# A two-layer decoder on one core: the feed forward begun in the tail of cross attention, with three smaller reorderings

## What is computed

```
x = x + gated_delta_net(layernorm(x))                # layer 0: recurrent attention, 8 heads
x = x + cross_attention0(layernorm(x), ctx, mask)    # 16 heads of 16
x = x + mixture_of_experts(layernorm(x))             # top 2 of 8 experts
x = x + self_attention(layernorm(x))                 # layer 1: causal, one head of 256
x = x + cross_attention1(layernorm(x), ctx, mask)    # 16 heads of 16, with biases
h = silu(xn @ w1 * s1) * (xn @ w2 * s2)              # xn = layernorm(x); ternary weights, 1024 hidden
h = gelu(h @ h1 * t1)                                # h1, h2: 1024 x 1024
h = gelu(h @ h2 * t2)
out = x + h @ w3 * s3
```

## Time and profile before

| what | value |
|---|---|
| executions (3) | 2084.59, 2084.89, 2089.97 us |
| profiled execution, its own time | 2085.05 us |
| its span in the trace | 2083.7 us |
| PE busy | 1951.1 us (94%) |
| DVE / ACT / POOL busy | 1124.0 / 689.5 / 624.0 us |
| mean granted TensorE clock | 0.981 of full |
| chain of waits, by engine | PE 78%, DVE 13%, issue 4%, ACT 2%, POOL 1%, DMA 1% |

### The profile page before, as it was taken

How to read it: one execution, slowest core, us unless ns; L and a number is a source line. 1 busy time by engine, 2 the same in 40 slices (tenths; PEclk the granted TensorE clock), 3 DMA queues, 4 the chain that set the end, 5 groups by cost and what they waited for, 6 DMA issues and landing times.

```text
span 2083.7 us, 38336 instructions
## 1 busy us (share of the span) xinstructions
PE 1951.1 (94%) x14432; PEld 1233.8 (59%) x14432; DVE 1124.0 (54%) x3161; ACT 689.5 (33%) x1720; POOL 624.0 (30%) x647
## 2 busy tenths in 40 slices
PE   6699999999888999998999899999889999999998
PEld 3467777777665666665445566666545545545545
DVE  6988888887655677676665566666520010100100
ACT  3134443443334555552001356555510110111100
POOL 3323333233104666663000266666500000000000
PEclk9899999999999999999999999999989999999999
DMA  5121211112103101010000000000030000000000
GB/s 171 26 26 23 33 21 27 29 20 28 15 11 114 34 24 34 23 32 10 0 0 1 9 27 19 26 19 27 2 162 0 9 0 0 9 0 0 9 0 9
DMA packets 126007, 53.73 MB, mean 26 GB/s; under 512 B 108680, under 2 KB 117760, under 8 KB 125056
## 3 DMA queue, kind: packets, MB, share of 16 engines
q1 hardware_dynamic: 125824, 51.27, 10.0%
HBM read 45.38 MB, written 5.85 MB: 25 GB/s over the span
## 4 chain that ended last, share of the span: by engine, by line
PE 78%; DVE 13%; issue 4%; ACT 2%; POOL 1%; DMA 1%; SPq 0%; DVEq 0%; ACTq 0%; POOLq 0%
PE ps L2103 19%; PE ps L515 6%; PE ps L1281 5%; PE ps L2090 5%; PE ps L1788 4%; PE ps L1303 4%; PE ps L1337 4%; PE ps L1358 3%; PE ps L1319 3%; PE ps L578 3%; PE ps L2111 3%; PE ps L639 2%; DVE big_b L783 2%; PE ps L1414 2%; PE ps L1290 1%
## 5 line engine op out<-in xcount | busy, mean ns | idle before, releaser
L1703 POOL TENSOR_TENSOR h_w<-h_w 125x336 int32<-125x336 int32 x384 | 337.5, 908 | 232.7 <-ACT h_w L1498 232.6
L1597 DVE CUSTOM_DVE_ANT_0 h_w<-ps,h_w 112x375 f32<-112x375 f32 x512 | 263.3, 543 | 3.1 <-PE ps L1281 3.0
L783 DVE SCALAR_TENSOR_TENSOR big_b<-ps,taps,big_b 128x444 f32<-128x444 f32 (+2 forms) x288 | 194.0, 674 | 26.8 <-ACT big_b L707 10.8
L1498 ACT ACTIVATE h_w<-ps 125x336 f32<-125x336 f32 x512 | 197.6, 468 | 22.2 <-PE ps L1303 22.2
L2103 PE MATMUL ps<-big_a,h_w 128*128 128x448 f32 x512 | 193.5, 540 | 3.7 <-DVE big_a L2150 3.7
L2103 PE MATMUL ps<-big_b,h_w 128*128 128x448 f32 x512 | 193.5, 540 | 0.7 <-ACT big_b L2129 0.7
L2158 DVE TENSOR_TENSOR xn<-ps,w_s 112x512 f32<-112x512 f32 x8 | 5.2, 686 | 299.4 <-PE ps L2111 299.4
L249 POOL TENSOR_TENSOR rstd<-var_eps,minus_half 112x4 f32<-112x4 f32 x12 | 12.1, 1011 | 488.4 <-DVE var_eps L236 488.4
L2103 PEld LDWEIGHTS ps<-big_a,h_w 128*128 128x128 f32 x512 | 97.0, 190 | 100.3 <-issue 93.7
L2103 PEld LDWEIGHTS ps<-big_b,h_w 128*128 128x128 f32 x512 | 96.9, 190 | 95.6 <-issue 93.7
L1303 PEld LDWEIGHTS ps<-h_w 32*125 32x125 f32 x3072 | 97.3, 185 | 61.9 <-issue 61.0
(11 more groups left out here) (230 smaller groups left out, 3385.5 us busy)
## 6 DMA issues: line engine op xcount, KB each, us to landing
h_w<-in_h SPq DMA_DIRECT2D x2, 4096.0 KB, 16.9
kq_w<-in_ctxT SPq DMA_DIRECT2D x16, 375.0 KB, 3.1
h_w<-in_ctxT SPq DMA_DIRECT2D x16, 375.0 KB, 3.3
h_w<-in_mask SPq DMA_DIRECT2D x16, 164.1 KB, 3.4
kq_w<-in_kq_w SPq DMA_DIRECT2D x8, 256.0 KB, 3.1
w<-in_vz_w SPq DMA_DIRECT2D x8, 256.0 KB, 3.4
blocks<-h_w SPq DMA_DIRECT2D x128, 12.2 KB
expert_w<-in_expert_w SPq DMA_DIRECT2D x1, 2048.0 KB
```

What stands on the lines that cost most here:

```text
L783: dve.scalar_tensor_tensor(p3(dst)[:, :, i:], p3(ps[:, bank, 0:GT])[:, :, 0:T - i], k.taps[:, h, n, TAPS - 1 - i:TAPS - i], p3(dst)[:, :, ...
L1498: act.activation(k.PTx[(4 * Q + r) % RING], ps[0:CK, turned_bank(Q, r), 0:NC * T], ACT.Exp).then_inc(s["exp"], 1)
L1597: dve.tensor_tensor_reduce(k.masked[r % 2], ps[0:T, score_bank(Q, r), 0:S2], k.mask_add[n % 2], -1.0, 3.0e38, ALU.add, ALU.min, k.neg_max[ ...
L1703: pool.tensor_tensor(P.bitcast(I32), P.bitcast(I32), k.mask_I[n % 2], ALU.mult).then_inc(s["weights"], 1)
```

## The change

Four edits.

1. **Feed forward begun in the tail.** In layer 1's cross attention the norm of feed forward's group 0 is done in the last sequence, in the places where layer 0 has the experts' norm (both of its copies on DVE). The first `BEGUN_FFN = 3` gate tiles are put at the ends of steps (B, 1), (B, 2) and (B, 3) on PE, two silus behind the copy of `oa` in (B, 2) on ACT, two products in (B, 2) and (B, 3) on DVE. In step (B, 1) `add_output(B - 2)` moves behind DVE's `weights`. PE's waits for `c_x` at the stage's start are gone; one stands now ahead of the next group's transposes. SP no longer waits for `c_x` ahead of h1 and h2, which have a semaphore each; `k.inv` gets memory of its own. `output_turn` and `output_back` of sequence B-2 wait for the norm's copies.
2. **Self-attention's norm on other banks.** Queries go to banks 4 and 5 and keys to 2 and 3 (`QK_BANKS`; before, queries had 2 and 3), and the next group's transposes go to banks 2 and 3, behind the waits for the copied queries and keys and no longer behind the copied values; that wait moves to `project_v`. PE's wait for `moe_x` moves from the stage's start to behind the first two projections, which use banks 4 and 5.
3. **First mask first.** `mask_rows(0)` stands ahead of the loop, so ahead of the first maxima, in both layers.
4. **Output by pairs.** `y_ps`, `y` and `ffn_x` count pairs of sequences: DVE scales and adds a pair when its products are done, SP sends eight transfers of two sequences where there were four of four.

```diff
@@ memory @@
+    k.inv = sb("inv", [T, XH])[:, :]
-    k.inv = room(XH, 1, parts=T)
@@ cross_pe: output_turn, output_back, early, loop @@
             pe.wait_ge(s["V"], 2 * n + 4)
             if l == 0:
                 pe.wait_ge(s["lnT_act"], LN_MOE + 1)
+            else:
+                pe.wait_ge(s["lnT_dve"], LN_FFN + 1)
...
-        if l == 0 and seq == B - 2:
-            pe.wait_ge(s["lnT_dve"], LN_MOE + 1)
+        if seq == B - 2:
+            pe.wait_ge(s["lnT_dve"], (LN_MOE + 1, LN_FFN + KD)[l])
...
-        elif l == 0 and (seq, q) == (B - 1, 2):
+        elif (seq, q) == (B - 1, 2):
             pe.wait_ge(s["V"], 2 * (n + 1))
-            ln_pe_half(pe, k, s, LN_MOE, 0, 7)
+            ln_pe_half(pe, k, s, LN_NEXT[l], 0, 7)
-        elif l == 0 and (seq, q) == (B - 1, 3):
+        elif (seq, q) == (B - 1, 3):
             pe.wait_ge(s["on"], n)
-            ln_pe_half(pe, k, s, LN_MOE, 1, 7)
+            ln_pe_half(pe, k, s, LN_NEXT[l], 1, 7)
...
+        elif l and (seq, q) == (B, 1):
+            pe.wait_ge(s["w_ffn"], 64)
+            pe.wait_ge(s["lnT_dve"], LN_FFN + KD)
+        if l and step in range(B * QUADS + 1, B * QUADS + 1 + BEGUN_FFN):
+            ffn_pe_gate(pe, k, s, 0, step - B * QUADS - 1)
@@ cross_act @@
+            elif l and seq == B:
+                act.wait_ge(s["w_ffn"], 64)
+                ffn_act_gate(act, k, s, 0, 0)
+                ffn_act_gate(act, k, s, 0, 1)
@@ cross_dve @@
+    mask_rows(0)
...
-        if q == 1 and is_sequence(seq - 2) and not (l == 0 and seq == B):
+        if q == 1 and is_sequence(seq - 2) and seq < B:
             add_output(seq - 2)
...
+        if l and (seq, q) in ((B - 1, 2), (B - 1, 3)):
+            ln_copy(dve, k, s, LN_FFN, q - 2, 7, k.xT[:, q - 2, :], "lnT_dve")
...
-        if q == 0 and seq == 0:
-            mask_rows(0)
...
+        elif (seq, q) == (B - 1, 0):
+            ln_dve_stats(dve, k, s, LN_FFN, 0)
+        elif (seq, q) == (B - 1, 1):
+            dve.wait_ge(s["xnT"], 2 * B)
+            ln_dve_scale(dve, k, s, LN_FFN, 0)
+        elif (seq, q) == (B, 1):
+            add_output(seq - 2)
+        elif (seq, q) == (B, 2):
+            dve.wait_ge(s["w_ffn"], 64)
+            ffn_dve_gate(dve, k, s, 0, 0)
+        elif (seq, q) == (B, 3):
+            ffn_dve_gate(dve, k, s, 0, 1)
@@ cross_pool @@
-        elif l == 0 and (seq, q) == (B - 1, 1):
-            ln_pool(pool, k, s, LN_MOE)
+        elif (seq, q) == (B - 1, 1):
+            ln_pool(pool, k, s, LN_NEXT[l])
@@ attention_pe @@
+QK_BANKS = (4, 5, 2, 3)
...
         for n in range(2 * KD):
+            if g == 0 and n == KD:
+                pe.wait_ge(s["moe_x"], 32 * NG)
             for c in range(KD):
-                ins = pe.matmul(ps[:, 2 + n, 0:GT], k.attn_w[:, c, n * 128:(n + 1) * 128], k.xT[:, c, :],
+                ins = pe.matmul(ps[:, QK_BANKS[n], 0:GT], k.attn_w[:, c, n * 128:(n + 1) * 128], k.xT[:, c, :],
...
-    pe.wait_ge(s["moe_x"], 32 * NG)
...
-        if more:
-            pe.wait_ge(s["v_sb"], g + 1)
-            ln_pe(pe, k, s, LN_ATTN + g + 1, 6)
         pe.wait_ge(s["q_sb"], 2 * (g + 1))
         pe.wait_ge(s["kk_sb"], 2 * (g + 1))
+        if more:
+            ln_pe(pe, k, s, LN_ATTN + g + 1, 2)
...
         if more:
+            pe.wait_ge(s["v_sb"], g + 1)
             project_v(g + 1)
@@ ffn_sp @@
-    sp.wait_ge(s["c_x"], 2 * B)
     sp.wait_ge(s["PV"], 2 * B * QUADS)
     for n in range(2):
-        sp.dma_start(k.hw[n][:, :, :], a[f"h{n + 1}"]).then_inc(s["hidden_w"], 16)
+        sp.dma_start(k.hw[n][:, :, :], a[f"h{n + 1}"]).then_inc(s[f"hidden_w{n}"], 16)
     for g in range(NG):
-        sp.wait_ge(s["ffn_x"], g + 1)
-        sp.dma_start(out[g].rearrange("b t d -> t b d"), k.x[:, g * G:g * G + G, :]).then_inc(s["out_done"], 16)
+        for n in range(2):
+            sp.wait_ge(s["ffn_x"], 2 * g + n + 1)
+            sp.dma_start(out[g, 2 * n:2 * n + 2].rearrange("b t d -> t b d"),
+                         k.x[:, g * G + 2 * n:g * G + 2 * n + 2, :]).then_inc(s["out_done"], 16)
@@ ffn_pe @@
+def ffn_pe_gate(pe, k, s, g, m):
+    if m >= 2:
+        pe.wait_ge(s["h0"], nth(g, HT, m - 2))
+    elif g:
+        pe.wait_ge(s["y"], 2 * g)
+    for n in range(2):
+        for c in range(KD):
+            ins = pe.matmul(k.ps[:, 2 + 2 * n + m % 2, 0:GT], ...)
+        ins.then_inc(s["w12"], 1)
...
-    pe.wait_ge(s["w_ffn"], 64)
-    pe.wait_ge(s["c_x"], 2 * B)
-    ln_pe(pe, k, s, LN_FFN, 6)
     for g in range(NG):
-        pe.wait_ge(s["lnT_dve"], LN_FFN + KD * g + KD)
+        if g:
+            pe.wait_ge(s["lnT_dve"], LN_FFN + KD * g + KD)
+        for m in range(0 if g else BEGUN_FFN, HT):
+            ffn_pe_gate(pe, k, s, g, m)
...
-                    pe.wait_ge(s["hidden_w"], 32)
+                if m == 0:
+                    pe.wait_ge(s[f"hidden_w{n}"], 16)
...
+                if g == 0:
+                    pe.wait_ge(s["c_x"], 2 * B)
                 ln_pe(pe, k, s, LN_FFN + g + 1, 6)
...
-        ins.then_inc(s["y_ps"], 1)
+            if j % 2:
+                ins.then_inc(s["y_ps"], 1)
@@ ffn_dve @@
-        dve.wait_ge(s["y_ps"], g + 1)
-        for n in range(G // 2):
...
+        for n in range(2):
+            dve.wait_ge(s["y_ps"], 2 * g + n + 1)
+            dve.tensor_tensor(y[:, 2 * n:2 * n + 2, :], two(ps[0:T, 4 + n, :]),
+                              k.w3_s[:, :].unsqueeze(1).to_broadcast([T, 2, D]), ALU.mult).then_inc(s["y"], 1)
+            dve.wait_ge(s["y"], 2 * g + n + 1)
+            xs = k.x[:, g * G + 2 * n:g * G + 2 * n + 2, :]
+            dve.tensor_tensor(xs, xs, y[:, 2 * n:2 * n + 2, :], ALU.add).then_inc(s["ffn_x"], 1)
```

More of the change, by code:

```diff
@@ L1085 @@
 POOL_BANKS = 6
+LN_NEXT = (LN_MOE, LN_FFN)
 def is_sequence(c):
@@ L1982, in queries @@
             act.wait_ge(s["qk"], nth(g, 4, n))
-            act.activation(qk[:, n, :], ps[:, 2 + n, 0:GT], ACT.Copy, scale=1.0 / 16).then_inc(s["q_sb"], 1)
+            act.activation(qk[:, n, :], ps[:, QK_BANKS[n], 0:GT], ACT.Copy, scale=1.0 / 16).then_inc(s["q_sb"], 1)
     def values(g):
@@ L2023, in attention_dve @@
         if g < NG - 1:
-            ln_copy(dve, k, s, LN_ATTN + g + 1, 1, 7, k.xT[:, 1, :], "lnT_dve")
+            ln_copy(dve, k, s, LN_ATTN + g + 1, 1, 3, k.xT[:, 1, :], "lnT_dve")
         dve.wait_ge(s["A_S"], g + 1)
@@ L2059, in attention_pool, with ffn_act_gate, ffn_dve_gate @@
     cross_norm_pool(pool, k, s, 1, 0)
+BEGUN_FFN = 3
 def ffn_sp(sp, k, s, a, out):
-    sp.wait_ge(s["c_x"], 2 * B)
     sp.wait_ge(s["PV"], 2 * B * QUADS)
     for n in range(2):
-        sp.dma_start(k.hw[n][:, :, :], a[f"h{n + 1}"]).then_inc(s["hidden_w"], 16)
+        sp.dma_start(k.hw[n][:, :, :], a[f"h{n + 1}"]).then_inc(s[f"hidden_w{n}"], 16)
     for g in range(NG):
-        sp.wait_ge(s["ffn_x"], g + 1)
-        sp.dma_start(out[g].rearrange("b t d -> t b d"), k.x[:, g * G:g * G + G, :]).then_inc(s["out_done"], 16)
+        for n in range(2):
[9 more added lines that the diff above has]
+        for c in range(KD):
+            ins = pe.matmul(k.ps[:, 2 + 2 * n + m % 2, 0:GT], k.w12[:, n, c, m * 128:(m + 1) * 128], k.xT[:, c, :],
+                            start=(c == 0), stop=(c == KD - 1))
+        ins.then_inc(s["w12"], 1)
+def ffn_act_gate(act, k, s, g, m):
+    act.wait_ge(s["w12"], nth(g, 2 * HT, 2 * m))
+    if m >= 2:
+        act.wait_ge(s["h0"], nth(g, HT, m - 2))
+    act.activation(k.silu[:, m % 2, :], k.ps[:, 2 + m % 2, 0:GT], ACT.Silu, scale=k.hid_s[:, 0, m:m + 1]).then_inc(s["silu"], 1)
+def ffn_dve_gate(dve, k, s, g, m):
+    dve.wait_ge(s["silu"], nth(g, HT, m))
+    dve.wait_ge(s["w12"], nth(g, 2 * HT, 2 * m + 1))
+    dve.scalar_tensor_tensor(k.big_a[:, m, :], k.ps[:, 4 + m % 2, 0:GT], k.hid_s[:, 1, m:m + 1], k.silu[:, m % 2, :],
+                             ALU.mult, ALU.mult).then_inc(s["h0"], 1)
 def ffn_pe(pe, k, s):
@@ L2118, in ffn_act @@
     layers = ((k.big_a, k.big_b), (k.big_b, k.big_a))
-    act.wait_ge(s["w_ffn"], 64)
     for g in range(NG):
-        for m in range(HT):
-            act.wait_ge(s["w12"], nth(g, 2 * HT, 2 * m))
-            if m >= 2:
-                act.wait_ge(s["h0"], nth(g, HT, m - 2))
-            act.activation(k.silu[:, m % 2, :], ps[:, 2 + m % 2, 0:GT], ACT.Silu, scale=k.hid_s[:, 0, m:m + 1]).then_inc(s["silu"], 1)
+        for m in range(0 if g else 2, HT):
+            ffn_act_gate(act, k, s, g, m)
         for n, (_, dst) in enumerate(layers):
@@ L2141, in transposed @@
             ln_copy(dve, k, s, LN_FFN + g, c, 6 + c, k.xT[:, c, :], "lnT_dve")
-    dve.wait_ge(s["w_ffn"], 64)
-    norm(0)
-    transposed(0)
     for g in range(NG):
-        for m in range(HT):
-            dve.wait_ge(s["silu"], nth(g, HT, m))
-            dve.wait_ge(s["w12"], nth(g, 2 * HT, 2 * m + 1))
-            dve.scalar_tensor_tensor(k.big_a[:, m, :], ps[:, 4 + m % 2, 0:GT], k.hid_s[:, 1, m:m + 1], k.silu[:, m % 2, :],
-                                     ALU.mult, ALU.mult).then_inc(s["h0"], 1)
```

(16 more changed lines are left out.)

16 lines of the change are left out of this document (3 added, 13 removed).

## The result

| | before | after | forecast |
|---|---|---|---|
| median of the runs, us | 2084.74 (2083.77 to 2089.97) | 2058.69 (2056.9 to 2059.98) | 2058.0 (2054.0 to 2065.5) |
| ratio, 95% interval | | 0.9869 [0.9851, 0.9888] | |
| profiled execution, its span | 2085.05, 2083.7 | 2056.9, 2055.6 | |

A forecast was written before the change was run, and what follows sets the result against it. PE's instruction list was taken as the bound, its idle or half-speed time as the gain. Edits 3, 2, 1 and 4 (seams, end) summed 6.4 + 2.7 + 14.05 + 2.0 + 1.9 = 27.05 us off 2085.05: 2058.0 us, range 2054.0 to 2065.5.

The forecast's parts named there:

- Sum 6.4: Cross attention's start in both layers: first mask ahead of the maxima gains 3.5 us in layer 0, 2.9 in layer 1.
- low end of 5.0: Cross attention's start in both layers: least gain expected of edit 3, whose high end was 7.3 us.
- 1180.3: Layer 1's cross attention: forecast start of L1303 in us, against 1183.26 before, a gain of 2.9.
- openings absorbed: Cross attention's first sequence: ACT's or POOL's queue takes back 5 of edit 3's 6.4 us; 2063 us, chance 0.11.
- high end of 2.8: Self-attention: most gain expected of edit 2, in us, whose low end was 1.3.
- 0.25 was charged: Layer 1's last sequence: cost in us of placing feed forward's norm there, at most 0.9.
- the high end, 15.4: Seam into feed forward: gain in us if filled slots keep the clock up before the drain.
- lower clock over the gates: Feed forward's group 0 gates: the lower clock level lasts over them, price 3.1 us, 2061.1 us; chance 0.15.
- Slower: Drain into h1: PE stays at half clock from 1505.7, for 67 us giving 2091.5 us; chance 0.02.
- no change: Start of h1 products: h1 lands after 1534.3, 27 us after issue, and PE waits; chance 0.02.
- DVE and POOL: Layer 1's last sequence: the two engines block each other more than in layer 0, 2 us, 2060 us; chance 0.08.
- the line between the earlier trace: Last output transfer: a line between 448 KB landing in 3.2 us and 98 KB in 1.7 gives 2.2 for 224 KB.

The follow-up runs named there:

- the nine profiles: Versions differing only in edit 3 from layer 0's first scores to layer 1's last: seven with it, mean 855.3 us; two without it, mean 858.9 us.
- the norm alone: Changed kernel with BEGUN_FFN = 0: norm stays in the last sequence, all eight gates come after the drain; median 2064.16 us.

## Why the prediction was right

**Bound.** PE's list was the right path: each edit's gain appeared at its own place, and left that place when the edit was undone. (That the stretches of the table sum to the whole shows nothing; they cover the span.)

**Edit 3, mis-sized.** The step that failed is "Sum 6.4": 4.15 in the two profiles, below even the low end of 5.0, 3.5 by the nine profiles, 2.6 and 4.9 in the medians when undone. The working took the gained time as start of L1303 before against after, and the sequence behind it as fixed. Two things were missed. First, the clock of these stretches differs between executions: a loosely filled stretch with the same instructions takes from 6.65 to 9.19 us. For layer 0 the forecast took 3.5, between full and half speed for the values products; for layer 1 its 1180.3 is full speed alone, and there the new L1361 is the slow one (3.35), so 1.60 came for 2.9. Second, 1.86 was lost again in layer 0's drain. That has the size of a part of the rival "openings absorbed", but not its cause: no queue of ACT or POOL took it within the first sequence; the lower level fell on other work, 320 us later. From the first L1306 to self-attention the versions that share edits 2 and 3 lie between 458.7 and 461.3 us. Two of them (edit 4 undone, the norm alone) take 458.7, with none of the loss, and of the two runs without edit 3 one takes 458.8, the other 459.9, with part of it. So the loss doesn't belong to the edit alone; what decides where the level falls there stays open.

**Edit 2, a little small.** Its mechanism came out wholly: both stops gone, and L1986 waiting for the add. 3.2 measured, above the high end of 2.8, for 2.7; the stops that come back when it is undone make 3.05. The start gave 1.3 for 1.14, since the first projections overlap the last expert product by 0.17 us, and the groups 1.9 for 1.57.

**Edit 1, right in its mechanism.** 15.3 against the kernel before and 14.2 when undone, for 14.05; the 1.1 between the two is for the most part how much of the lower level the version without the edit happened to see. Gates between L1322, L1401, L1410 and L1419, normalize under gate 1, table load in the slack, h1 in time, and 0.23 of idle behind DVE's statistics, 0.40 from start to start, where 0.25 was charged. One step of the working gave nothing: the forecast let the last L1319 start 0.9 earlier because `add_output` no longer stands ahead of DVE's mask product. It starts 2.39 after the output before it; with edit 1 undone it is 2.41, a wait of 1.27 for POOL instead of 1.29 for DVE. What came of it in the pair is clock, since that output took 2.05 before and 1.12 after. The forecast let the lower level last until 1506.3; it did not come at all in this stretch. That was the case of the high end, 15.4. The rival "lower clock over the gates" is what the version with the norm alone shows: 0.52 for 7 us, once the three gates are out of the drain. So the gates in the drain do two things, they fill 2.35 us of stops and save 3.1 us of half-speed work, and the forecast had the second only as a rival's price (3.1). "Slower" and "no change" needed 54 us of lower level and 27 us of landing; there were 0 and 12.4. (The 48 us of landing that "no change" gives for 2085 is a slip: 27 until PE meets h1 and 27 lost make 54.)

**DVE and POOL.** The price of 2 us for each blocking the other did not come: L242 in the last sequence takes 1.38 for its four, its value without POOL in the earlier trace rows, though POOL multiplies in the same step. Taken one by one, the rows show what decided: the fourth scaling of the earlier trace rows starts at 948.71, 0.03 behind a product of POOL's, and takes 1.02, its three fellows 0.40 each; here it starts at 1482.09, 0.16 ahead of POOL's product, and takes 0.40 too. So whether this price comes hangs on less than 0.2 us. No run moved the one against the other.

**Edit 4.** 4.2 for 3.9. The seams gave 2.15 (2.0), DVE at the end 1.1 (1.2), the transfer 0.9 (0.7): 224 KB land in 2.3 us where the line between the earlier trace rows gave 2.2. The estimate from the Trainium skill's figures (DMA: Bandwidth & Descriptors, "Anatomy of one DMA") was 0.5 for it, and the measurement decides: 0.9.

So the mechanism was right, and that the total came within 0.7 us is luck: 2.25 too much in edit 3 stands against 1.25 + 0.5 + 0.3 too little elsewhere, and the 1.3 us ahead of the first scores, which no edit touches, is within what executions of one kernel differ by (2057.89 to 2063.38 in one set of four).
